# Two stages of a four-layer kernel reordered: the layer-0 attention body and the layer norm inside the layer-1 ternary feed-forward

## The chip, the cores and the metric

The kernel runs as one program on one core of a Trainium2 chip. The metric is the device time of that program in microseconds (us), as the median of several runs. The engines that matter are TensorE (PE in the profile), VectorE (DVE), ScalarE (ACT), GpSimd (POOL) and SyncE (SP, which issues the transfers). Each engine works through its own instructions in program order. Engines wait for each other on semaphores.

## The reference

The reference is a stack of four layers over `x` of 4 batches x 512 rows x 512 features, each with a cross-attention part and a feed-forward part, both added to `x` with a tanh gate. Two parts matter here.

```python
# layer 0 attention (teacher_logits is layernorm(x), teacher_features is the context)
query  = einsum('bnc,dc->bnd', teacher_features, Wq) + bq
key    = einsum('bnc,dc->bnd', teacher_features, Wk) + bk
attention = softmax(einsum('bnd,bmd->bnm', query, key), axis=-1)
x = x + tanh(g_xattn[0]) * einsum('bln,bmn->blm', teacher_logits, attention)

# layer 1 feed-forward
def act_quant(x):                       # per row, 8 bits
    scale = 128 / clip(max(abs(x), axis=-1), 1e-5)
    return clip(round(x * scale), -128, 127) / scale
def bitlinear(x, w):   return einsum('bsh,oh->bso', act_quant(x), weight_quant(w))
def h_bitlinear(x, w): return einsum('bsh,oh->bso', act_quant(fwht(x)), weight_quant(w))
x = x + tanh(g_ffn[1]) * h_bitlinear(silu(bitlinear(n, w_gate)) * bitlinear(n, w_up), w_down)   # n = layernorm(x)
```

Layer 3's attention slot is a selective scan. It needs, from the context alone, a projection, a causal convolution of four taps with silu (`u`), a small projection (`xd`) and `dt = softplus(...)`. The kernel computes these inside the layer-0 attention stage, beside the attention.

## The kernel before

The program is a chain of phases, each ended by a barrier over all engines: `setup`, `l0_xattn`, `l0_ffn`, `l1_xattn`, `l1_ffn`, `l2_xattn` and so on. The change touches `l0_xattn` (line 345), `l1_ffn` (line 1472) and the class `LayerNorm` (line 131). Inside a phase the order on each engine is written out by hand. PSUM banks are handed round by a `Ring`: a list of jobs in order, each job taking the next bank, with a semaphore for "filled" and one for "drained". A job that is to fill a bank waits until the earlier job on that bank has been drained.

**`l0_xattn`** loops over four batches b (a body). On PE a body transposes the normalised rows (`xt`), makes `q` and `k`, projects `u` to `xd` (`project_x`), makes four score tiles `e0` to `e3`, then `dt` tiles, transposes the probabilities (`pt`), and makes four output tiles `out0` to `out3`, with the input projections of the next batch (`in{b+1}_c`) in between. The score tiles wait for `q` (drained by ACT) and `k` (drained by DVE). DVE takes the maximum of each score tile, ACT takes the exponential, DVE scales, PE transposes. DVE further does the convolution of the next batch (`convolve`, four pieces c), the layer norm of the next batch and the residual additions. Softplus is a chain across three engines: ACT takes small_exp, logarithm, inverse, then GpSimd multiplies (line 671), ACT squares, and DVE closes with five passes per piece (`softplus(b, c)`, lines 611 and 615). Before the change the body of b ends on DVE with `softplus(b, 0)` and `softplus(b, 1)`, ahead of the `xt` and `k` drains of b+1, and pieces 2 and 3 come after the `pt` copies of b+1. On ACT a body ends with `gated(b + 1)`, the silu that makes `u`.

**`l1_ffn`** is a software pipeline over 16 row tiles t (T1 = 16, four per batch). In turn t, PE transposes `mid` of t-1, makes gate and up of t, transposes the quantised rows of t-3, does half of the Hadamard transform of t-1 (line 1574), the down product of t-3, and the other half of the transform. DVE in turn t does, in this order: `widest(t-2)`, which drains the transform's banks; `rest(t-2)`, three butterfly passes, the row maximum and the scale; `middle(t)`, which is silu(gate) times up; and `down(t-3)`, the residual. `widest` must drain two banks before PE can transpose the last of `mid`. ACT copies, takes the silu, and rounds the transformed rows in `y_round(t-2)`. Once per batch there is extra work for the next batch. At t % 4 == 1 DVE runs the whole layer norm behind `down`. At t % 4 == 2 it runs `quantise_x` there: the row maximum, the scale, then two clamping passes into `tmp` for each of four tiles. At t % 4 == 3 ACT turns `tmp` into the integers `xq` in one pass behind `y_round` (`x_round`). At t % 4 == 0 PE transposes `xq` and ACT copies the result to `xqt`.

Of the kernel before, what the change touches and what calls it, by code (L numbers as in the profile page):

```python
# [9 lines left out]
ALU = mybir.AluOpType  # L10
ACT = mybir.ActivationFunctionType
# [124 lines left out]
class LayerNorm:  # L136
# [10 lines left out]
    def vector(self, dve, i, batch, xn_free, xn=None, first=0):  # L147
        g, st = self.g, self.steps
        xn = g["xn"] if xn is None else xn
# [17 lines left out]
        xn_free()  # L167
# [177 lines left out]
def l0_xattn(nc, g, a, early):  # L345

    with Phase(nc, "l0x") as ph:
# [79 lines left out]
        def _(pe):  # L427
# [28 lines left out]
            for b in range(NB):  # L456
# [29 lines left out]
        def _(act):  # L486
# [36 lines left out]
            def small_exp(b):  # L523
                for c in range(DC):
# [5 lines left out]
            def logarithm(b):  # L530
                for c in range(DC):
# [3 lines left out]
            def inverse(b):  # L535
                for c in range(DC):
# [3 lines left out]
            def squares(b):  # L540
                for c in range(DC):
# [9 lines left out]
            for b in range(NB):  # L551
# [17 lines left out]
                small_exp(b)  # L569
                pad(b + 1, 2)  # L570
                logarithm(b)
                pad(b + 1, 3)
                inverse(b)
                squares(b)
                gated(b + 1)

        @blk.vector
        def _(dve):
# [42 lines left out]
            for b in range(NB):  # L621
                xt_drain(dve, "dve", g, ring, b, xt)
                ring.wait_filled(dve, b, "k")
                ring.drain(dve.tensor_scalar(kt[:], bank("k"), bias[:, 1:2], None, ALU.add), "k")
                for m in range(ST):
# [12 lines left out]
                convolve(b + 1, 0)  # L638
# [3 lines left out]
                if b > 0:  # L642
                    softplus(b - 1, 2)
                    softplus(b - 1, 3)
# [3178 lines left out]
```

## Time and profile before

| what | us |
|---|---|
| median of 3 runs (3500.46 to 3504.72) | 3502.61 |
| the profiled execution, own time | 3490.28 |
| its span, first to last instruction | 3488.6 |

In the profiled execution, `l0_xattn` runs from about 15 us to 232 us, and `l1_ffn` from 1077 us to about 1450 us. Times inside the trace are us from the start of the span. In a timeline row the first number is the start, the second the duration of the group up to the end of its last instruction, "xN" the number of instructions in it, and the bracket says how long the engine had been idle before it and what released it. Back-to-back instructions overlap a little, so busy time is not exactly elapsed time.

### The profile page before, as it was taken

How to read it: one execution, taken by the hardware profiler on the slowest of the kernel's cores; microseconds unless marked ns; L12 is line 12 of the kernel's file. 1: busy time of each engine (PE TensorE's matmuls, PEld its weight loads, DVE VectorE, ACT ScalarE, POOL GpSimd, SP SyncE). 2: the span in 40 equal slices, each digit the busy share in tenths (PEclk: the TensorE clock that was granted, in tenths of full speed). 3: DMA queues.
4: the chain of work that ended last, by engine and by line, in shares of the span. 5: the costliest groups of instructions: out<-in, count | busy, mean ns of one | idle time of the engine just before them, and what ended most of it. 6: DMA issues, size and time to landing. Idle time of an engine off the chain costs nothing. (4 is left out here: it accounts for less than half of the span.)

```text
span 3488.6 us, 42689 instructions
## 1 busy us (share of the span) xinstructions
PE 3122.0 (89%) x14213; PEld 1833.0 (53%) x14244; DVE 2621.1 (75%) x3478; ACT 1844.0 (53%) x3430; POOL 1443.2 (41%) x957
## 2 busy tenths in 40 slices
PE   7869797999997888799999999999999787998985
PEld 3437554333334555455555555555555366786663
DVE  7855689877774888468888888887788864765886
ACT  5644343666663655565666666666656432664220
POOL 1122279000000000067777777777778654223430
PEclk9879899999998999899999999999999898999998
DMA  4137735222216400245555555455454346675421
GB/s 133 40 118 277 277 103 151 58 58 58 64 32 150 63 1 1 85 153 155 182 170 167 162 189 168 154 169 180 159 171 144 127 182 211 249 254 192 145 73 60
DMA packets 229749, 478.66 MB, mean 137 GB/s; under 512 B 36239, under 2 KB 69647, under 8 KB 213664
## 3 DMA queue, kind: packets, MB, share of 16 engines
q1 hardware_dynamic: 223296, 459.19, 41.2%
q0 software_dynamic: 6240, 16.81, 1.3%
q8 instruction: 113, 1.85, 0.2%
q14 instruction: 100, 0.82, 0.1%
HBM read 387.51 MB, written 92.06 MB: 137 GB/s over the span
## 5 line engine op out<-in xcount | busy, mean ns | idle before, releaser
L2393 POOL TENSOR_TENSOR l2x_inflow<-l2x_dtu,l2x_rows_b 128x512 f32<-128x512 f32 x256 | 437.2, 1708 | 254.8 <-DVE l2x_state L2279 253.5
L178 POOL TENSOR_TENSOR ln_work<-ln_work,minus_half 128x4 f32<-128x4 f32 (+1 forms) x34 | 33.1, 975 | 1000.4 <-DVE ln_work L166 1000.3
L2279 DVE TENSOR_TENSOR_SCAN l2x_state<-l2x_decay,l2x_inflow 128x512 f32<-128x512 f32 x256 | 403.9, 1578 | 0.0
L2409 POOL TENSOR_TENSOR l2x_y_sum<-l2x_y_sum,l2x_state 128x512 f32<-128x512 f32 x224 | 387.0, 1728 | 29.2 <-DVE l2x_state L2288 29.2
L1324 DVE TENSOR_REDUCE l1x_mx<-psum 128x2 f32<-128x1024 f32 x256 | 308.4, 1219 | 96.6 <-PE psum L1166 95.2
L1281 ACT ACTIVATE l1x_split<-psum 128x1024 f32<-128x1024 f32 x256 | 262.0, 1025 | 155.6 <-PE psum L1166 155.6
L2288 DVE TENSOR_TENSOR l2x_state<-l2x_state,l2x_rows_c 128x512 f32<-128x512 f32 x256 | 298.2, 1165 | 7.1
L2151 ACT ACTIVATE l2x_decay<-l2x_dt,a_neg 128x512 f32<-128x512 f32 x256 | 181.6, 721 | 165.5 <-DVE l2x_state L2279 165.1
L126 PE MATMUL psum<-l2x_probs_t,l2x_v_tok 128*128 128x512 f32 x512 | 236.3, 605 | 16.1 <-ACT l2x_qt L212 12.9
L126 PE MATMUL psum<-l2x_xt,l2x_wq 128*128 128x512 f32 x512 | 231.9, 597 | 8.6 <-issue 8.6
L2086 ACT ACTIVATE l2x_probs<-psum,l2x_soft,l2x_norms 128x512 f32<-128x512 f32 x256 | 195.6, 774 | 79.9 <-DVE l2x_soft L2218 79.9
L126 PE MATMUL psum<-l2x_kt,l2x_qt 128*128 128x512 f32 x512 | 228.7, 593 | 0.9 <-DVE x_res L218 0.9
L126 PE MATMUL psum<-l2x_wo,l2x_ot 128*128 128x512 f32 x512 | 222.5, 592 | 0.9 <-DVE l2x_ot L2230 0.9
L126 PE MATMUL psum<-l2x_wkv,l2x_ctx_t 128*128 128x512 f32 x768 | 199.1, 415 | 8.8 <-DMA l2x_wkv<-l2x_kv_dram 8.8
L2211 DVE TENSOR_REDUCE l2x_soft<-psum 128x1 f32<-128x512 f32 x256 | 163.5, 681 | 34.9 <-PE psum L126 34.7
L126 PEld LDWEIGHTS psum<-l2x_wkv,l2x_ctx_t 128*128 128x128 f32 x768 | 146.4, 191 | 55.7 <-issue 13.9
L1190 PE MATMUL psum<-l1x_split,l1x_v 128*32 128x256 f32 x2048 | 164.2, 393 | 2.4 <-ACT l1x_o_sb L212 1.3
L126 PEld LDWEIGHTS psum<-l2x_xt,l2x_wq 128*128 128x128 f32 x512 | 96.3, 191 | 126.0 <-issue 125.8
L126 PEld LDWEIGHTS psum<-l2x_wo,l2x_ot 128*128 128x128 f32 x512 | 96.0, 190 | 116.5 <-issue 116.5
L126 PEld LDWEIGHTS psum<-l2x_probs_t,l2x_v_tok 128*128 128x128 f32 x512 | 93.2, 192 | 115.9 <-issue 93.5
L126 PEld LDWEIGHTS psum<-l2x_kt,l2x_qt 128*128 128x128 f32 x512 | 94.4, 190 | 103.6 <-issue 91.6
L119 PEld LDWEIGHTS psum<-ident,l2x_probs 128*128 128x128 f32 x1024 | 115.9, 143 | 47.5 <-issue 37.0
(459 smaller groups left out, 7147.5 us busy)
## 6 DMA issues: line engine op xcount, KB each, us to landing
l2x_rows_b<-l3x_xd_dram SPq DMA_DIRECT2D x256, 256.0 KB, 3.9
l2x_rows_c<-l3x_xd_dram SPq DMA_DIRECT2D x256, 256.0 KB, 3.5
l2w_raw<-l_w SPq DMA_DIRECT2D x38, 1024.0 KB, 6.7
l2x_wkv<-l2x_kv_dram SPq DMA_DIRECT2D x32, 1024.0 KB, 6.8
l2w_raw<-l_w SPq DMA_DIRECT2D x38, 512.0 KB, 4.7
l1x_heads_dram<-l1x_stage SPq DMA_DIRECT2D x32, 512.0 KB, 3.3
l2x_wq<-l_wq SPq DMA_DIRECT2D x16, 1024.0 KB, 5.1
l2x_wo<-l_wo SPq DMA_DIRECT2D x16, 1024.0 KB, 7.3
```

The lines of the kernel that those rows point to most:

```text
L119: last = pe.transpose(bank[:, k * P:(k + 1) * P], tile, ident)
L126: last = pe.matmul(out, lhsT, rhs, start=(k == 0), stop=(k == len(pairs) - 1))
L1190: last = pe.matmul(bank(f"o{gg}", outr)[32 * j:32 * j + 32, cols], v[:, gg // NG, kt, h * VW:h * VW + 2 * HD], probs[:, kt % 2, j, cols], ...
L1281: main.drain(act.activation(probs[:, kt % 2, 2 * j:2 * j + 2, :], g["psum"][:, b:b + 2, :], ACT.Exp, scale=HD ** -0.5), f"{job}_0", banks=2)
L1324: main.drain(dve.tensor_reduce(mx[:, gg % 2, :, j, t], g["psum"][:, b:b + 2, :], AX.X, ALU.max), f"m{n}_0", banks=2)
L2086: ring.drain(act.activation(probs[:, h % 2, t, :], bank(f"s{u}_{h}_{t}"), ACT.Exp, bias=soft[:, h, 1, t:t + 1], scale=norms[:, u % 2, 1, h ...
L2151: act.activation(decay[:, s % 3, :], dt[:, u % 2, :], ACT.Exp, scale=g["a_neg"][:, u % G2, n:n + 1]).then_inc(decay_ready, 1)
L2211: dve.tensor_reduce(soft[:, h, 0, t:t + 1], bank(f"s{u}_{h}_{t}"), AX.X, ALU.max, negate=True).then_inc(max_ready, 1)
L2279: dve.tensor_tensor_scan(state[:, s % KEPT, :], decay[:, s % 3, :], inflow[:, s % 3, :], 0.0, ALU.mult, ALU.add).then_inc(scan_done, 1)
L2288: dve.tensor_tensor(tile, tile, rows_c[:, s % 3, :], ALU.mult).then_inc(gathered, 1)
L2393: pool.tensor_tensor(inflow[:, s % 3, :], dtu[:], rows_b[:, s % 3, :], ALU.mult).then_inc(inflow_ready, 1)
L2409: pool.tensor_tensor(total, total, state[:, s % KEPT, :], ALU.add).then_inc(added, 1)
```

## The change

In `l0_xattn`, for bodies b > 0: PE makes the score tiles before `project_x`. ACT takes `gated(b)` after the `q` drain instead of at the end of body b-1, and takes `xd` after the exponentials. `project_in(b+1, 0)` and its `pad` come before the first `dt` tiles. DVE runs `softplus(b-1, 0)` behind the `xt` drains, `softplus(b-1, 1)` behind the `k` drain, pieces 2 and 3 ahead of the `pt` copies; `convolve(b+1, 0)` comes behind these copies and `convolve(b+1, 1)` into the gap in the layer norm. In the last body ACT runs the softplus chain in two halves of two pieces, and DVE runs pieces 0 and 1 ahead of the residual additions.

In `l1_ffn`: the layer norm is cut into `moments` (at t % 4 == 0) and `apply` (at t % 4 == 1). These and `quantise_x` (at t % 4 == 2) now stand between `widest` and `rest`. `quantise_x` loses its passes over `tmp`; ACT does them in `x_round`, as four scaled activations and one Relu pass that clamps, and the turned copy undoes the sign. `x_round` stands ahead of `y_round`.

```diff
@@ LayerNorm
     def vector(self, dve, i, batch, xn_free, xn=None, first=0):
+        self.moments(dve, i, batch, first)
+        xn_free()
+        self.apply(dve, i, batch, xn, first)
...
@@ l0_xattn
-            jobs += [f"xd{b}", f"dt{b}_0", f"dt{b}_1", ins[0], f"dt{b}_2", ins[1], f"dt{b}_3", ins[2], ins[3]]
+            jobs += [f"xd{b}", ins[0], f"dt{b}_0", f"dt{b}_1", f"dt{b}_2", ins[1], f"dt{b}_3", ins[2], ins[3]]
...
@@ l0_xattn, PE
-                project_x(b)
+                if b == 0:
+                    project_x(b)
                 for m in range(ST):
                     ring.wait_for(pe, b, free=f"e{m}", drained=["q", "k"])
                     ring.fill(product(pe, bank(f"e{m}"), [(qt[:, m * P:(m + 1) * P], kt[:])]))
+                if b > 0:
+                    project_x(b)
+                project_in(b + 1, 0)
                 project_dt(b, 0)
                 project_dt(b, 1)
-                project_in(b + 1, 0)
                 project_dt(b, 2)
...
@@ l0_xattn, ACT
-                take_xd(b)
+                if b > 0:
+                    gated(b)
+                if b == 0:
+                    take_xd(b)
...                                     # the four exponentials
+                if b > 0:
+                    take_xd(b)
+                pad(b + 1, 0)
                 signs(b, 0)
                 signs(b, 1)
-                pad(b + 1, 0)
...
-                squares(b)
-                gated(b + 1)
+                if b < NB - 1:
...                                     # the chain as before, over all four pieces
+                else:
+                    for pieces in ((0, 1), (2, 3)):
+                        small_exp(b, pieces)
+                        logarithm(b, pieces)
+                        inverse(b, pieces)
+                        squares(b, pieces)
...
@@ l0_xattn, DVE
                 xt_drain(dve, "dve", g, ring, b, xt)
+                if b > 0:
+                    softplus(b - 1, 0)
                 ring.wait_filled(dve, b, "k")
                 ring.drain(dve.tensor_scalar(kt[:], bank("k"), bias[:, 1:2], None, ALU.add), "k")
+                if b > 0:
+                    softplus(b - 1, 1)
...
-                convolve(b + 1, 0)
+                if b > 0:
+                    softplus(b - 1, 2)
+                    softplus(b - 1, 3)
+                else:
+                    convolve(b + 1, 0)
...                                     # pt copies
                 if b > 0:
-                    softplus(b - 1, 2)
-                    softplus(b - 1, 3)
+                    convolve(b + 1, 0)
...
-                ln.vector(dve, b, (b + 1) % NB, lambda: ring.wait_filled(dve, b, "xt3"))
-                convolve(b + 1, 1)
-                convolve(b + 1, 2)
+                def xn_free(b=b):
+                    convolve(b + 1, 1)
+                    ring.wait_filled(dve, b, "xt3")
+
+                ln.vector(dve, b, (b + 1) % NB, xn_free)
+                if b == NB - 1:
+                    softplus(b, 0)
+                    softplus(b, 1)
...                                     # out0, out1
+                convolve(b + 1, 2)
                 convolve(b + 1, 3)
...                                     # out2, out3
-                softplus(b, 0)
-                softplus(b, 1)
...
@@ l1_ffn, ACT
             def x_round(b):
                 act.wait_ge(x_ready, b + 1)
+                for s in range(ST):
+                    act.activation(tmp[:, s, :], g["xn"][:, s, :], ACT.Copy, scale=xs[:, b % 2, 2, s:s + 1],
+                                   bias=ROUND).then_inc(x_rounded, 1)
+                act.wait_ge(x_rounded, (b + 1) * ST)
...
-                act.activation(xq[:]..., tmp[:]..., ACT.Copy, bias=-ROUND).then_inc(xq_done, 1)
+                act.activation(xq[:]..., tmp[:]..., ACT.Relu, scale=-1.0, bias=top[:, 0:1]).then_inc(xq_done, 1)
...
                 if 0 <= t - 1 < T1:
                     halves(t - 1)
+                if t % ST == ST - 1 and t // ST + 1 < NB:
+                    x_round(t // ST + 1)
                 if 0 <= t - 2 < T1:
                     y_round(t - 2)
-                if t % ST == ST - 1 and t // ST + 1 < NB:
-                    x_round(t // ST + 1)
@@ l1_ffn, DVE
...                                     # quantise_x: two clamping passes per tile and their waits removed
+                b = t // ST
                 if 0 <= t - 2 < T1:
                     widest(t - 2)
+                if t % ST == 0 and t < T1:
+                    if b == NB - 1:
+                        ring.wait_for(dve, 0, drained=[f"dn{ST - 1}"])
+                    ln.moments(dve, b, (b + 1) % NB)
+                if t % ST == 1 and t < T1:
+                    dve.wait_ge(xq_done, b + 1)
+                    ln.apply(dve, b, (b + 1) % NB)
+                if t % ST == 2 and b + 1 < NB:
+                    ln.wait_xn(dve, b + 1)
+                    quantise_x(b + 1)
+                if 0 <= t - 2 < T1:
                     rest(t - 2)
                 if t < T1:
                     middle(t)
                 if 0 <= t - 3 < T1:
                     down(t - 3)
-                b = t // ST
...                                     # the layer norm and quantise_x that stood here are gone
```

## Rows read from the trace of the kernel before

**Rows 1.** The page: the span, and the busy time of each engine.
```profile
span 3488.6 us, 42689 instructions
PE 3122.0 (89%) x14213; PEld 1833.0 (53%) x14244; DVE 2621.1 (75%) x3478; ACT 1844.0 (53%) x3430; POOL 1443.2 (41%) x957
```
**Rows 2.** Busy time by stretch: length, then PE, PEld, DVE, ACT, POOL, clock, DMA share.
```profile
132.22:183.20 50.98, 43.65 (x113) 19.20 (x113) 43.73 (x72) 30.49 (x50) 7.10 (x5) 0.90 0.11 43
183.20:228.15 44.95, 26.67 (x65) 12.36 (x64) 36.29 (x63) 22.82 (x38) 7.02 (x5) 0.76 0.06 25
1077.00:1450.00 373.00, 295.23 (x1837) 190.36 (x1869) 299.28 (x432) 204.25 (x238) 4.63 (x7) 0.90 0.27 50
```
**Rows 3.** Timeline of PE in the attention: the score tiles of bodies 1, 2, 3.
```profile
79.72 3.70 PE L126 MATMUL psum<-l0x_kt,l0x_qt 128*128 128x512 f32 x8 [0.63 <-DVE l0x_kt L624]
...
132.22 3.70 PE L126 MATMUL psum<-l0x_kt,l0x_qt 128*128 128x512 f32 x8
...
183.20 3.70 PE L126 MATMUL psum<-l0x_kt,l0x_qt 128*128 128x512 f32 x8
```
**Rows 4.** Waits in the attention, 15 to 232 us: total, times, longest.
```profile
DVE l0x_conv L594 <- ACT l0x_padded L212: 12.7, 4, 4.3
```
**Rows 5.** Timeline of DVE in the attention: two convolution pieces, and the last instruction.
```profile
109.73 2.33 DVE L597 SCALAR_TENSOR_TENSOR l0x_conv<-l0x_padded,early_conv_w,l0x_conv 128x512 f32<-128x512 f32 x3
...
112.49 5.00 DVE L597 SCALAR_TENSOR_TENSOR l0x_conv<-l0x_padded,early_conv_w,l0x_conv 128x512 f32<-128x512 f32 x3
...
227.46 0.69 DVE L615 SCALAR_TENSOR_TENSOR l0x_dt<-l0x_small,l0x_relu 128x512 f32<-128x512 f32 x1
```
**Rows 6.** Timeline of ACT in the last body of the attention.
```profile
207.62 1.28 ACT L538 ACT_TABLE_LOAD   x1
208.91 2.19 ACT L538 ACTIVATE l0x_ratio<-l0x_magnitude 128x512 f32<-128x512 f32 x4
```
**Rows 7.** Waits in the feed-forward, 1077 to 1450 us.
```profile
PE psum L119 <- DVE l1f_z L1735: 41.8, 12, 6.1
```
**Rows 8.** Timeline of PE, feed-forward: the transform that closes a turn.
```profile
1156.62 1.95 PE L1574 MATMUL psum<-l1f_had,l1f_mid_t 128*128 128x128 f32 x16
...
1304.11 1.95 PE L1574 MATMUL psum<-l1f_had,l1f_mid_t 128*128 128x128 f32 x16
...
1328.23 1.95 PE L1574 MATMUL psum<-l1f_had,l1f_mid_t 128*128 128x128 f32 x16
...
1347.62 1.95 PE L1574 MATMUL psum<-l1f_had,l1f_mid_t 128*128 128x128 f32 x16
...
1364.94 1.95 PE L1574 MATMUL psum<-l1f_had,l1f_mid_t 128*128 128x128 f32 x16
...
1389.55 1.95 PE L1574 MATMUL psum<-l1f_had,l1f_mid_t 128*128 128x128 f32 x16
...
1406.87 1.95 PE L1574 MATMUL psum<-l1f_had,l1f_mid_t 128*128 128x128 f32 x16
```
**Rows 9.** Timeline of DVE in the feed-forward.
```profile
1304.98 2.28 DVE L1693 TENSOR_REDUCE l1f_xs<-xn 128x4 f32<-128x2048 f32 x1
...
1307.98 1.67 DVE L1704 TENSOR_SCALAR l1f_tmp<-xn,l1f_xs 128x512 f32<-128x512 f32 x4
...
1347.83 0.75 DVE L1759 SCALAR_TENSOR_TENSOR x_res<-psum,l1f_ys,x_res 128x512 f32<-128x512 f32 x1 [2.88 <-PE psum L126]
...
1365.81 2.46 DVE L154 BATCH_NORM_STATS2 ln_stats<-x_res 128x6 f32<-128x512 f32 x4
...
1370.52 1.92 DVE L171 TENSOR_SCALAR xn<-x_res,ln_work 128x512 f32<-128x512 f32 x4 [1.23 <-POOL ln_work L178]
...
1407.07 0.75 DVE L1759 SCALAR_TENSOR_TENSOR x_res<-psum,l1f_ys,x_res 128x512 f32<-128x512 f32 x1 [0.81 <-PE psum L126]
```
**Rows 10.** Timeline of ACT at a batch boundary of the feed-forward.
```profile
1243.91 1.89 ACT L1617 ACTIVATE l1f_xq<-l1f_tmp 128x2048 bf16<-128x2048 f32 x1
1246.52 1.94 ACT L212 ACTIVATE l1f_xqt<-psum 128x1024 bf16<-128x1024 bf16 x2 [0.71 <-PE psum L1543]
```

More of the change, by code:

```diff
@@ L147, in vector, with moments @@
     def vector(self, dve, i, batch, xn_free, xn=None, first=0):
+        self.moments(dve, i, batch, first)
+        xn_free()
+        self.apply(dve, i, batch, xn, first)
+    def moments(self, dve, i, batch, first=0):
         g, st = self.g, self.steps
-        xn = g["xn"] if xn is None else xn
         st.begin(i)
@@ L166, in vector, with apply @@
         dve.tensor_scalar(w[:, 6, :], w[:, 3, :], 0.5, None, ALU.mult).then_inc(self.var_ready, 1)
-        xn_free()
+    def apply(self, dve, i, batch, xn=None, first=0):
+        g, st = self.g, self.steps
+        xn = g["xn"] if xn is None else xn
+        w = g["ln_work"][:, :, first:first + self.tiles]
         dve.wait_ge(self.var_ready, i * 2 + 2)
@@ L521, in signs, with small_exp @@
                 side.drain(act.activation(relu[:, b % 2, c, :], bank(job, side), ACT.Relu, bias=dt_b[:, c:c + 1]), job)
-            def small_exp(b):
-                for c in range(DC):
+            def small_exp(b, pieces):
+                for c in pieces:
                     if b > 0:
@@ L528, in small_exp, with logarithm, inverse, squares @@
                     act.activation(small[:, c, :], magnitude[:, b % 2, c, :], ACT.Exp, scale=-1.0).then_inc(exp_done, 1)
[L530 to L531 removed]
+            def logarithm(b, pieces):
+                for c in pieces:
                     act.wait_ge(exp_done, b * DC + c + 1)
                     act.activation(magnitude[:, b % 2, c, :], small[:, c, :], ACT.Ln, bias=two[:, 0:1]).then_inc(ln_done, 1)
[L535 to L536 removed]
+            def inverse(b, pieces):
+                for c in pieces:
                     act.wait_ge(ln_done, b * DC + c + 1)
                     act.activation(ratio[:, c, :], magnitude[:, b % 2, c, :], ACT.Exp, scale=-1.0).then_inc(ratio_exp, 1)
[L540 to L541 removed]
+            def squares(b, pieces):
+                for c in pieces:
                     act.wait_ge(ratio_done, b * DC + c + 1)
@@ L1614, in x_round @@
                 act.wait_ge(x_ready, b + 1)
+                for s in range(ST):
+                    act.activation(tmp[:, s, :], g["xn"][:, s, :], ACT.Copy, scale=xs[:, b % 2, 2, s:s + 1],
+                                   bias=ROUND).then_inc(x_rounded, 1)
+                act.wait_ge(x_rounded, (b + 1) * ST)
                 if b >= 1:
                     ring.wait_filled(act, 0, f"xq{b - 1}_1")
-                act.activation(xq[:].rearrange("p s d -> p (s d)"), tmp[:].rearrange("p s d -> p (s d)"), ACT.Copy,
-                               bias=-ROUND).then_inc(xq_done, 1)
+                act.activation(xq[:].rearrange("p s d -> p (s d)"), tmp[:].rearrange("p s d -> p (s d)"), ACT.Relu,
+                               scale=-1.0, bias=top[:, 0:1]).then_inc(xq_done, 1)
             def x_turned(b):
@@ L1622, in x_turned @@
                     ring.wait_filled(act, 0, f"xq{b}_{k}")
-                    copy(act, "act", ring, f"xq{b}_{k}", xqt[:, b % 2, 2 * k:2 * k + 2, :].rearrange("p c n -> p (c n)"),
-                         bank_bf(f"xq{b}_{k}"))
+                    ring.drain(act.activation(xqt[:, b % 2, 2 * k:2 * k + 2, :].rearrange("p c n -> p (c n)"),
+                                              bank_bf(f"xq{b}_{k}"), ACT.Copy, scale=-1.0, bias=QMAX), f"xq{b}_{k}")
             def middle_turned(t):
@@ L1698, in quantise_x @@
                 xst.wait(dve)
+                dve.sem_inc(x_ready, 1)
                 dve.tensor_scalar(v[:, 4, :], v[:, 1, :], w_abs[:, 0, 0:1], None, ALU.mult).then_inc(scaled, 1)
                 dve.tensor_scalar(v[:, 5, :], v[:, 1, :], w_abs[:, 0, 1:2], None, ALU.mult).then_inc(scaled, 1)
-                if b >= 1:
-                    dve.wait_ge(xq_done, b)
-                for s in range(ST):
-                    xst.inc(dve.tensor_scalar(tmp[:, s, :], g["xn"][:, s, :], v[:, 2, s:s + 1], QMAX, ALU.mult, ALU.min))
-                xst.wait(dve)
-                for s in range(ST - 1):
-                    xst.inc(dve.tensor_scalar(tmp[:, s, :], tmp[:, s, :], QMIN, ROUND, ALU.max, ALU.add))
-                xst.wait(dve)
-                s = ST - 1
-                dve.tensor_scalar(tmp[:, s, :], tmp[:, s, :], QMIN, ROUND, ALU.max, ALU.add).then_inc(x_ready, 1)
             def middle(t):
@@ L1770, in _ @@
                     down(t - 3)
-                b = t // ST
-                if t % ST == 1 and t < T1:
-                    if b == NB - 1:
-                        ring.wait_for(dve, 0, drained=[f"dn{ST - 1}"])
-                    ln.vector(dve, b, (b + 1) % NB, lambda: dve.wait_ge(x_ready, b + 1))
-                if t % ST == 2 and b + 1 < NB:
-                    ln.wait_xn(dve, b + 1)
-                    quantise_x(b + 1)
         @blk.gpsimd
```

14 lines of the change are left out of this document (8 added, 6 removed).

## The prediction, on record before the result was known

> **What bounds the kernel now.** I read the page first. PE is busy 89% of the span and DVE 75% [rows 1], but these are averages over ten phases, and the change touches two. So the next view is busy time by stretch. One body of the attention, from the score tiles of batch 2 to those of batch 3, takes 50.98 us, in which PE is busy 43.65 and DVE 43.73 [rows 2]. Neither engine fills the body: each stands for some 7 us of it, waiting for the other. The feed-forward takes 373 us, with PE busy for 295 and DVE for 299 [rows 2]. Again two engines with nearly equal work take turns.
>
> The waits say where. In the feed-forward PE waited 41.8 us in 12 waits for DVE's `widest` (the last subtraction, line 1735) [rows 7]. The timeline of PE gives the rhythm. I take the start of the transform that closes each turn [rows 8]: 1304.11, 1328.23, 1347.62, 1364.94, 1389.55, 1406.87. The differences are 24.12 (the turn behind `quantise_x`), 19.39 (a batch boundary), 17.32 (plain), 24.61 (behind the layer norm), 17.32 (plain). A plain turn is PE's own loop: DVE still waits 0.81 us for the down product in it [rows 9]. Layer norm and quantisation each add about 7 us to a turn, because they stand on DVE between `down` and `widest`, exactly where PE waits for the banks.
>
> In the attention DVE's longest-lasting wait is for the padded input of the convolution, 12.7 us in four waits [rows 4], and the score tiles of bodies 1 to 3 start at 79.72, 132.22 and 183.20 [rows 3], so bodies of 52.50 and 50.98 us, and 44.95 from the last score tiles to the last DVE instruction at 228.15 [rows 3, 5].
>
> **The change part by part: feed-forward.** Nothing of the plain turn changes, so 17.32 stays. The extra pieces now stand between `widest` and `rest`, behind the drain for which PE waits. They delay `rest` and `middle`, and only what exceeds DVE's slack in that turn comes onto the path.
> - t % 4 == 1, `apply`: 1.92 us [rows 9]. DVE's slack in a plain turn is 0.81, to some 1.05 with the short wait behind `down`. So +0.8: 18.1 us. GpSimd's power, which costs a wait of 1.23 now, is a turn old by then and costs nothing.
> - t % 4 == 2, `quantise_x`: what remains runs from 1304.98 to 1307.98, 3.0 us [rows 9]. Less the slack: +2.0, so 19.3 us. The clamping passes that leave DVE are the 3.2 us that follow.
> - t % 4 == 3: plain for DVE, 17.3 us.
> - t % 4 == 0, `moments`: from 1365.81 to 1370.52 less the 1.23 of waiting, 3.5 us [rows 9]. DVE waits 2.88 at a boundary now [rows 9]. The boundary itself gets longer on ACT, which now does x_round's four activations and y_round before it copies `xqt`. Four activations of 128x512 take 2.19 [rows 6], and the Relu pass I price as today's pass, 1.89 [rows 10]. PE's transposes of `xq`, for which ACT now waits 0.71 [rows 10], are hidden beside y_round. So +2.2 - 0.7 = +1.5, which raises DVE's slack to 4.4 and covers the 3.5 of `moments`. The turn: 20.9 us. Were the four activations free it would be +0; were y_round's delay to add in full, +2.2.
>
> A batch: 20.9 + 18.1 + 19.3 + 17.3 = 75.6. Before, from 1156.62 to 1328.23 two batches took 171.61 [rows 8], so 85.8 each: two gains of 10.2. The last batch has no `quantise_x`: 20.9 + 18.1 + 17.3 + 17.3 = 73.6 against 78.64 (1328.23 to 1406.87): 5.0. In the first three turns the layer norm (3.5 + 1.2 + 1.9) and the quantisation (3.0 + 3.2) stand in line the same way, 12.8 us. DVE is the bound there, so the 3.0 that remains stays: 9, between 6 and 10. The run-out behind 1406.87 is untouched. Sum: 20.4 + 5.0 + 9 = 34 us, between 25 and 37.
>
> What queues behind the moved work: behind the longer x_round stands y_round of the same turn. Its result is wanted by PE only after the next turn's gate and up products, more than half a turn later, so the 4.1 us are hidden; without that cover they would come on top at each of three boundaries, 12 us. The start of the stage waits for weights by DMA, so the first x_round costs nothing.
>
> **The change part by part: attention.** No work leaves DVE, so a body can't be shorter than its 43.7 us of DVE work [rows 2]. What the order does is to give DVE something to do where it waits. One softplus piece is five passes of 0.69 [rows 5], 3.5 us. Piece 0 covers the time in which PE makes `q` and `k`, piece 1 the time until the first score tile, pieces 2 and 3 (7 us) the time in which ACT signs the `dt` tiles and PE transposes, and convolution 0 starts when its input has long been padded, so the 12.7 us of [rows 4] mostly go. On PE the score tiles no longer stand behind `project_x`, which waits for ACT's silu. In exchange they wait for `k` behind softplus piece 0: about 2.5 us of idle PE. Laid out by the durations of the trace, PE's own loop then takes 43 to 44, DVE's 43.7. I take 44.8, since part of PE's work will run at the lower of its two clocks as now (granted 0.90 of 2.4 GHz over body 2 [rows 2]); that puts PE some 1 us behind DVE. Bounds: 43.7 and 50.
>
> - Body 1: 52.50 to 44.8, -7.7. Body 2: 50.98 to 44.8, -6.2.
> - Score tiles of body 1: one softplus piece (3.5) moves from ahead of them to behind them, and body 0 gains about 1.5 where convolution 0 no longer waits for its padding: -5.
> - Last body: DVE has 36.3 us of work in its 44.95 [rows 2]. It gets the 3.5 that moved behind the score tiles, 39.8. It keeps the 1.2 wait for GpSimd in the layer norm and about 1 us before piece 0 of its own softplus: 42, -3. The halves add two table loads of 1.28 [rows 6] to ACT, which lie ahead of pieces 2 and 3, while DVE does pieces 0 and 1 and four residuals. Without this cover they would cost 2.6.
> - GpSimd's multiplies will still slow DVE next to them: three convolution passes took 5.00 instead of 2.33 [rows 5]. I leave that as it is, +-3 us in all.
>
> Sum: 7.7 + 6.2 + 5 + 3 = 22 us, between 10 and 27. SP's stores of `u`, `xd` and `dt` keep their order and have slack; the last store still follows the last softplus.
>
> The row of a table load shows it at 207.62 for 1.28 us and the next activation at 208.91, right behind it [rows 6]. The Trainium skill, "ScalarE: Activation LUTs", section "What ACT_TABLE_LOAD costs", puts a switch at about 2.66 us, since a drain comes on top of the load. By that rule two more switches cost 5.3 us instead of 2.6, of which my layout hides about 2, and the total would be some 3 us worse. The trace doesn't agree: it has no such gap.
>
> **Sum.** 34 + 22 = 56 us. The profiled execution took 3490.28 (span 3488.6), so it would come to 3434. The median of the runs stands 12.3 above it, at 3502.61. I apply the same difference: 3447 us.
>
> **The rivals.**
> - *Only the feed-forward gains.* In the attention PE's granted clock and the new wait for `k` eat the gaps: three bodies at 50 us. For it: DVE and PE are equally loaded, and each new order has new handovers. Against: DVE's waits of [rows 4] have a clear cause. Time: 3502.6 - 34 = 3469.
> - *Only the attention gains.* If `rest` and y_round are late for PE's transposes, each inserted piece (3.5 + 1.9 + 3.0 a batch) comes back onto the path. Against: the down product's wait shows slack only of 0.81, but the y rows are made most of a turn ahead. Time: 3502.6 - 22 = 3481, less what the removed 3.2 us save.
> - *Slower: the attention falls to the lower clock.* PE stands before every set of score tiles, and in the last body, which has such gaps, the granted clock is 0.76 [rows 2]. If bodies 1 to 3 ran at 0.6, PE's 43.65 us at 0.90 would become 65.5, with 3.5 of waiting 69 against 51: +18 a body, +54, less 34: 3523. It decides from about 0.67, where +11 a body eats the feed-forward's 34. Against: today's body 2 keeps 0.90 with as much idle time as the new one.
> - *The change doesn't do what it says:* PE's loop in both stages has other links that I missed, and all comes back as waits: within 7 us of 3502.6.
>
> **How the numbers follow.** Forecast, both stages gain (3436 to 3458): 0.76. Only the feed-forward: 0.12. Only the attention: 0.06. Nothing: 0.03. Lower clock: 0.03. Range: from the best case of both terms (37 + 27 = 64, less 2 for the runs' spread: 3436) to the feed-forward alone, 3470. About 0.2% (7 us) is what a measurement of this kernel can tell from no change. Faster 0.94, same 0.03, slower 0.03.
>
> **What would show it.** In the profile after: the waits of PE for `widest` fall from 41.8 to a few us; turns of 17.3, 18.1, 19.3 and 20.9 between the closing transforms; `xqt` copies right behind y_round at a boundary; bodies of about 45 us between score tiles, and convolution 0 without a wait; the last softplus pass of the attention near 205. I am wrong in the feed-forward if plain turns are no longer 17.3 or the y transposes wait for ACT, and in the attention if PE's waits before the score tiles are well over 3 us or its clock there is below today's.

## The result and the profile after

The changed kernel takes 3452.74 us (median of 4 runs, 3448.78 to 3460.69), against 3501.53 before in the same session. The ratio is 0.9866, 95% interval 0.9843 to 0.9888: 48.8 us less. The forecast was 3447, and 56 us less. The profiled execution took 3448.78.

The page after; as [rows 1]:
```profile
span 3447.1 us, 42710 instructions
PE 3117.6 (90%) x14244; PEld 1829.8 (53%) x14244; DVE 2600.7 (75%) x3446; ACT 1857.3 (54%) x3448; POOL 1444.7 (42%) x957
```
The busy sums hardly move (PE -4, DVE -20, ACT +13), while the span falls by 41.5. What went is idle time, so the waits and the turns tell more than the sums.

The score tiles of the attention after, from PE's timeline, as [rows 3], then DVE's last instruction, as in [rows 5]:
```profile
36.86 3.70 PE L126 MATMUL psum<-l0x_kt,l0x_qt 128*128 128x512 f32 x8
75.71 3.70 PE L126 MATMUL psum<-l0x_kt,l0x_qt 128*128 128x512 f32 x8 [1.07 <-DVE l0x_kt L648]
120.14 5.40 PE L126 MATMUL psum<-l0x_kt,l0x_qt 128*128 128x512 f32 x8 [2.32 <-DVE l0x_kt L648]
166.01 3.70 PE L126 MATMUL psum<-l0x_kt,l0x_qt 128*128 128x512 f32 x8 [2.32 <-DVE l0x_kt L648]
...
207.84 0.69 DVE L637 SCALAR_TENSOR_TENSOR l0x_dt<-l0x_small,l0x_relu 128x512 f32<-128x512 f32 x1
```
Bodies 1 and 2 went from 52.50 and 50.98 to 44.43 and 45.87 us. The last part, from the last score tiles to the end of the last softplus pass, went from 44.95 to 42.52. The attention ends at 208.53 instead of 228.15: 19.6 us earlier, where 22 were forecast. The new wait for `k` is there, in brackets.

The waits in the attention after, 15 to 232 us (total, times, longest), where the first is that of [rows 4]:
```profile
DVE l0x_conv L616 <- ACT l0x_padded L220: 4.1, 1, 4.1
PE psum L126 <- DVE l0x_kt L648: 5.7, 3, 2.3
```
The 4.1 us that are left for the padded input are at 21.34, ahead of the first score tiles; between the bodies that wait is gone.

The feed-forward's closing transforms, as [rows 8] (L1574 is now L1609), from that of turn 3 to that of turn 7:
```profile
1132.80 1.95 PE L1609 MATMUL psum<-l1f_had,l1f_mid_t 128*128 128x128 f32 x16
...
1155.73 1.95 PE L1609 MATMUL psum<-l1f_had,l1f_mid_t 128*128 128x128 f32 x16
...
1173.05 1.95 PE L1609 MATMUL psum<-l1f_had,l1f_mid_t 128*128 128x128 f32 x16
...
1191.30 1.95 PE L1609 MATMUL psum<-l1f_had,l1f_mid_t 128*128 128x128 f32 x16
...
1210.76 1.95 PE L1609 MATMUL psum<-l1f_had,l1f_mid_t 128*128 128x128 f32 x16
```
The turns are 22.93 (boundary), 17.32 (plain), 18.25 (`apply`), 19.46 (`quantise_x`). The next two boundaries take 21.24 and 22.92, and the other turns repeat to 0.01. From the stage's first load to the closing transform at 1362.83 (before: 1406.87) it is 303.06 us instead of 329.51: 26.5 less, where 34 were forecast. PE's waits there, as [rows 7]:
```profile
PE psum L119 <- DVE l1f_z L1765: 8.7, 18, 0.5
PE psum L119 <- ACT l1f_xqt L1662: 7.8, 6, 2.4
PE psum L119 <- DVEq L1754: 7.4, 4, 5.1
```
The 41.8 us in 12 waits for `widest` have become 8.7 in 18, none over 0.5. Two waits have grown. One is for `xqt`, 2.35 and 0.26 us at each of three boundaries, where none was over 0.3 before. The other is for DVE's `middle` (line 1754): `quantise_x` now stands ahead of it, and at the start of the stage, where DVE has no slack, PE waits 5.10 us for it in turn 3. Before, that wait was one of 1.0 us:
```profile
PE psum L119 <- DVEq L1724: 1.0, 1, 1.0
```

### The profile page after: what moved, and what is told of

Same layout as the page of the kernel before. It is cut to its first block and busy times, and to the rows that moved or that the text cites. A ratio compares the mean times of both kernels' runs of the same rounds, so it can differ in the third digit from the quotient of the medians.

```text
span 3447.1 us, 42710 instructions
## 1 busy us (share of the span) xinstructions
PE 3117.6 (90%) x14244; PEld 1829.8 (53%) x14244; DVE 2600.7 (75%) x3446; ACT 1857.3 (54%) x3448; POOL 1444.7 (42%) x957
## 3 DMA queue, kind: packets, MB, share of 16 engines
q1 hardware_dynamic: 223296, 459.19, 41.8%
```

## The experiments

Below, "the stage" is the feed-forward from its first load to the closing transform one turn ahead of the last one named above: 312.2 us before, 285.7 after. Kernels marked "one execution" ran once. The same code can differ by some us between executions: the seven kernels here that have the changed feed-forward (the changed kernel, e1 and a1 to a5) took 282.9 to 285.8 for this stage. From the closing transform of turn 3 on they agree within 0.1 us, so nearly all of that spread lies in the first four turns.

**e1_ffn_only.** The feed-forward's part of the change alone; `l0_xattn` is that of before.

> The feed-forward part of the change alone, attention as before. If the two parts are independent, the feed-forward stage keeps what it has with the whole change (303.1 us from its first instruction to the closing transform of turn 15, against 329.5 before) and the attention keeps its 228; median about 26 below before, so near 3476. If one stage's order or clock carries over into the other, the stage would be off by more than 2 us.

Measured: 3473.07 (4 runs), ratio 0.9931 [0.9905, 0.9957], 28.6 us less. The attention is as before (bodies 52.81 and 50.91), the stage is 284.0. The theory of independent parts holds.

**e2_attn_only.** The attention's part alone; `l1_ffn` is that of before.

> The attention part alone, feed-forward as before. Independent parts: the last softplus of the attention ends near 208.5 (228.2 before), the feed-forward stage is 329.5 again, the median about 20 below before, near 3482. The two medians' gains add up to the whole change's 49 within the runs' spread of some 5.

Measured: 3474.13 (6 runs), ratio 0.9933 [0.9915, 0.9952], 27.5 us less. Bodies 44.30 and 44.36, last part 42.41, the stage 313.1. The gain is larger than the 20 expected, and than the 18.1 us by which the attention ended earlier in the profiled execution (at 210.07). The two halves add up to 56.1 against 48.8 for the whole. Each of the three gains has an interval of some 6 to 9 us to either side, so no interaction is seen. Both rivals with one half without gain fall.

**e3_old_place.** The feed-forward's extra pieces back behind `down`; ScalarE still rounds, so the clamping passes stay gone. ("..." marks lines left out.)
```diff
                     widest(t - 2)
-                if t % ST == 0 and t < T1:
...
-                    ln.moments(dve, b, (b + 1) % NB)
-                if t % ST == 1 and t < T1:
...
-                    ln.apply(dve, b, (b + 1) % NB)
-                if t % ST == 2 and b + 1 < NB:
...
-                    quantise_x(b + 1)
...
                     down(t - 3)
+                if t % ST == 1 and t < T1:
...
+                    ln.vector(dve, b, (b + 1) % NB, lambda: dve.wait_ge(xq_done, b + 1))
+                if t % ST == 2 and b + 1 < NB:
...
+                    quantise_x(b + 1)
```


> The whole change, but layer norm and quantisation stand behind the down residual again, in one piece each; the rounding stays on ScalarE. Theory (the place is what gains): the layer-norm turn is 24.6 again, the quantisation turn 24.1 - 3.2 = 20.9, the boundary 21.2 to 22.9, a plain turn 17.3, a batch 84 to 86, and the stage up to the closing transform of turn 15 about 323 to 327, so next to nothing of the 26 us is left. Rival (the 3.2 us a batch taken off VectorE is what gains, here counted with what hangs on it): the stage stays below 312.

Measured (one execution): 3474.63; the stage 315.1, so nothing of its gain is left. PE's waits in it:
```profile
PE psum L119 <- DVE l1f_z L1765: 35.2, 18, 5.9
PE psum L119 <- ACT l1f_xqt L1662: 7.8, 6, 2.4
```
The wait for `widest` is back. The turns are 21.2 to 22.9 (boundary), 17.3 (plain), 24.8 to 25.9 (behind the layer norm) and 20.1 to 21.5 (behind `quantise_x`). DVE is rid of 3.2 us of passes a batch, which makes the last of these 2.8 to 4.0 shorter than before; the boundary, with the passes on ScalarE, is 1.8 to 3.5 longer. The theory's side is right, though the stage up to turn 15 took 332.4, over its 323 to 327.

**e4_dve_passes.** The reverse: the new place, with the clamping passes on DVE and one rounding pass on ScalarE behind `y_round`, as before. The main part of its edit:
```diff
...
+                for s in range(ST):
+                    xst.inc(dve.tensor_scalar(tmp[:, s, :], g["xn"][:, s, :], v[:, 2, s:s + 1], QMAX, ALU.mult, ALU.min))
...
-                for s in range(ST):
-                    act.activation(tmp[:, s, :], g["xn"][:, s, :], ACT.Copy, scale=xs[:, b % 2, 2, s:s + 1], bias=ROUND)
```


> The whole change, but the clamping passes are VectorE's again and ScalarE rounds in one pass behind y_round, as before; the pieces stand at their new places. Theory (the place gains): the boundary is 19.4 again, the turn with apply 18.3, the turn with quantisation 17.3 - 1.0 + 6.2 = 22.5, plain 17.3, a batch 77.5 against 76.3 to 78.0 with the change, the stage 302 to 306. Rival (the passes taken off VectorE gain): the stage is above 315.

Measured (one execution): 3462.87; the stage 288.5, 24 of the 26 us. The boundaries take 19.39, the turns behind them 17.65, the `quantise_x` turns 23.4 and 25.0, where 22.5 was expected. Moving the passes to ScalarE takes 4 to 5.5 us from one turn and puts 2 to 3.5 on another.

**e5_y_first.** On every fourth turn `y_round` stands ahead of `x_round`.
```diff
-                if t % ST == ST - 1 and t // ST + 1 < NB:
-                    x_round(t // ST + 1)
                 if 0 <= t - 2 < T1:
                     y_round(t - 2)
+                if t % ST == ST - 1 and t // ST + 1 < NB:
+                    x_round(t // ST + 1)
```


> The changed kernel, with ScalarE's two rounding helpers swapped on every fourth turn of the ternary feed-forward: y_round of the turn stands ahead of x_round of the next batch. Theory (the boundary turn is set by ScalarE's queue, in which the four scaled activations and the Relu pass, 2.57 + 2.00, delay the next evictions of h, and by the transposes of xqt behind them): the Relu pass of y, 2.00, and its move now stand ahead of x's, so xqt comes about 2 us later, TensorE waits about 2 us longer at each boundary, and the boundary turn goes from 21.2 to 22.9 up to 23 to 25; plain, quantise and apply turns stay at 17.3, 19.4 and 18.3; the stage from its first load to the closing transform of turn 14 goes from 285.7 to about 291 to 294. Rival (the order of the two is free, since both have slack and the boundary is set by the layer norm on VectorE): no turn differs by more than 0.3 and the stage stays at 286.

Measured (one execution): 3454.08; boundaries 24.17, 23.26, 23.95 (+1.0 to +2.0, +4.3 in all), all turns between and behind them the same. The boundaries lie in the range expected, with somewhat over half of the 2 us each on average: the boundary does hang on when `xqt` is made. The stage, 288.1, is below the 291 to 294 expected, also because its first four turns took 71.1 here and 73.0 in the changed kernel.

**e6_gaps.** The four scaled activations leave ScalarE's block; each stands behind one silu of the last turn of a batch.
```diff
             def x_round(b):
-                act.wait_ge(x_ready, b + 1)
-                for s in range(ST):
...
+                    if s == ST - 1 and b + 1 < NB:          # behind silu n of turn t
+                        if n == 0:
+                            act.wait_ge(x_ready, b + 2)
+                        x_scaled(b + 1, n)
```


> The changed kernel, with the four scaled activations of x_round taken out of its block and set one by one behind the silus of the last turn of a batch; its Relu pass stays in its place. Theory (the boundary is set by ScalarE's block of 2.57 + 2.00 between two sets of evictions, and by the wait for xqt that ends TensorE's activity and lowers its clock): xqt comes 2 to 2.6 us earlier, TensorE's waits of 2.35 at the boundaries go, the clock stays at its upper level behind them, and the boundary turn goes from 21.2 to 22.9 down to 19.3 to 20.5; the stage to turn 14's closing transform from 285.7 to 277 to 281. Rival (the scaled activations between silus delay each silu by 0.64, and with it the elementwise product and the next transforms, on a turn that TensorE sets): the last turn of each batch is 1 to 2.6 longer in exchange, and the stage stays at 285 to 287.

Measured (one execution): 3441.12; all three boundaries 18.66, the turns right behind them 18.38 (+1.06), the last turn of a batch unchanged, the stage 275.7. That is 10.0 us better, of which 2.1 lie in the first four turns (71.0), within what those turns vary by with the changed kernel's feed-forward. From turn 3 on it is 7.9 us better, where all executions of the changed feed-forward agree.

The +1.06 is DVE's slack used up, and not the rival's delayed silus. Here is DVE's first residual behind the first boundary, in the changed kernel and in e6:
```profile
1155.93 0.75 DVE L1789 SCALAR_TENSOR_TENSOR x_res<-psum,l1f_ys,x_res 128x512 f32<-128x512 f32 x1 [3.02 <-PE psum L126]
...
1149.52 0.75 DVE L1796 SCALAR_TENSOR_TENSOR x_res<-psum,l1f_ys,x_res 128x512 f32<-128x512 f32 x1
```
In the long boundary DVE waits 3.02 us for it, so the 3.5 us of `moments` are covered. In the short one it waits for nothing, and what `moments` has too much comes onto the next turn. The same kernel was timed again over several executions:

> The kernel with the four scaled activations between the silus of the last turn of a batch, timed in rounds (its one look gave 3441.1, with a stage 10.0 us shorter than the changed kernel's 285.7 and layer norms, attention and layer-1 mixer as there). Theory (the boundaries were the part of the feed-forward's forecast that was missing): a median of 3438 to 3446, a ratio to before of 0.982 to 0.984, and the boundary turns again at 18.4 to 19.0. Rival (the one look was a lucky execution): 3449 to 3456, as the changed kernel.

Measured: 3443.82 (4 runs, 3435.22 to 3446.61), ratio 0.9855 [0.9838, 0.9871]; boundaries 18.65 to 18.66, the stage 277.3. Its median and its boundaries are in the range expected, its ratio is just above it. Its median is 8.9 below the changed kernel's, but the kernel before ran 7.7 faster beside it too, and the intervals of the two ratios overlap. The 7.9 us behind turn 3 are 8.0 here; that the whole kernel is faster than the changed one isn't shown. Of the timed kernels it has the lowest ratio.

ScalarE at the first boundary, in its timeline, the changed kernel:
```profile
1130.04 2.57 ACT L1651 ACTIVATE l1f_tmp<-xn,l1f_xs 128x512 f32<-128x512 f32 x4
1132.64 2.00 ACT L1656 ACTIVATE l1f_xq<-l1f_tmp,l1f_top 128x2048 bf16<-128x2048 f32 x1
1134.55 1.99 ACT L1689 ACTIVATE l1f_z<-l1f_z,l1f_ys 128x2048 f32<-128x2048 f32 x1
1136.57 2.00 ACT L1693 ACTIVATE l1f_yq<-l1f_z,l1f_top 128x2048 bf16<-128x2048 f32 x1
1138.48 1.92 ACT L1662 ACTIVATE l1f_xqt<-psum 128x1024 bf16<-128x1024 bf16 x2
```
And with the gaps filled (b1_gaps_5), where the closing transform starts at 1132.65:
```profile
1120.57 0.69 ACT L1678 ACTIVATE l1f_silu<-psum,l1f_xs 128x512 f32<-128x512 f32 x1 [1.16 <-PE psum L126]
1121.16 0.71 ACT L1649 ACTIVATE l1f_tmp<-xn,l1f_xs 128x512 f32<-128x512 f32 x1
1122.35 0.69 ACT L1678 ACTIVATE l1f_silu<-psum,l1f_xs 128x512 f32<-128x512 f32 x1 [0.48 <-PE psum L126]
...
1129.89 2.02 ACT L1656 ACTIVATE l1f_xq<-l1f_tmp,l1f_top 128x2048 bf16<-128x2048 f32 x1
1131.78 2.02 ACT L1693 ACTIVATE l1f_z<-l1f_z,l1f_ys 128x2048 f32<-128x2048 f32 x1
1133.83 2.00 ACT L1697 ACTIVATE l1f_yq<-l1f_z,l1f_top 128x2048 bf16<-128x2048 f32 x1
1135.74 1.00 ACT L1662 ACTIVATE l1f_xqt<-psum 128x1024 bf16<-128x1024 bf16 x1
```
The first `xqt` copy starts 3.1 us behind the closing transform instead of 5.7. What PE does with that, first in the changed kernel:
```profile
1139.54 0.66 PE L119 MATMUL psum<-ident,l1f_mid 128*128 128x128 f32 x4 [2.35 <-ACT l1f_xqt L1662]
1140.45 0.66 PE L119 MATMUL psum<-ident,l1f_mid 128*128 128x128 f32 x4 [0.26 <-ACT l1f_xqt L1662]
1140.94 1.71 PE L126 MATMUL psum<-l1f_w_gate,l1f_xqt 128*128 128x512 bf16 x4
1142.44 1.91 PE L126 MATMUL psum<-l1f_w_up,l1f_xqt 128*128 128x512 bf16 x4
```
Then with the gaps filled:
```profile
1137.71 0.66 PE L119 MATMUL psum<-ident,l1f_mid 128*128 128x128 f32 x4 [0.24 <-ACT l1f_xqt L1662]
...
1139.08 1.03 PE L126 MATMUL psum<-l1f_w_up,l1f_xqt 128*128 128x512 bf16 x4
1139.94 1.03 PE L126 MATMUL psum<-l1f_w_gate,l1f_xqt 128*128 128x512 bf16 x4
```
Behind the waits of 2.35 and 0.26 four matmuls take 1.91 us, the lower of the clock's two levels; behind 0.24 they take 1.03, the upper. The second boundary of the changed kernel has the same two waits, and its matmuls take 1.03: it is the one of 21.24 us.

**a1_k_first.** The attention with the eviction of `k` ahead of the first softplus piece.
```diff
-                if b > 0:
-                    softplus(b - 1, 0)
                 ring.wait_filled(dve, b, "k")
                 ring.drain(dve.tensor_scalar(kt[:], bank("k"), bias[:, 1:2], None, ALU.add), "k")
                 if b > 0:
+                    softplus(b - 1, 0)
                     softplus(b - 1, 1)
```


> The changed kernel, with the first piece of the previous body's softplus chain behind the eviction of k in VectorE's order instead of ahead of it. Theory (VectorE sets the bodies of the layer-0 attention): TensorE's wait for k of 2 to 3 us a body goes, VectorE's work is the same, and the bodies stay at 44.4 and 45.9 within 1 us. Rival (the wait of TensorE for k is on the path): the two middle bodies get 1.5 to 2.5 shorter each, 3 to 5 in all, and the first score tile of the next bodies comes as much earlier.

Measured (one execution): 3463.68; bodies 46.46 and 45.44, last part 47.91. It is worse, as neither said. Waits in its last part:
```profile
ACT l0x_probs L572 <- DVE l0x_neg_max L652: 4.0, 1, 4.0
PE psum L126 <- ACT l0x_xd L220: 3.7, 1, 3.7
```
The piece now stands with its neighbour ahead of the first maximum, ScalarE's exponentials wait 4.0 us for that (2.2 in the changed kernel), `xd` behind them is late, and PE waits 3.7 for it. With `k` first PE still waits 0.85 us for it at each body, where it waited 1.07 to 2.32. So a piece ahead of `k` costs PE 0.2 to 1.5 us; behind it, it costs the softmax chain more.

**a4_dve_order and a5_pe_act_order.** The attention's new order split by engine: VectorE's alone (TensorE and ScalarE as before, last chain undivided), and its complement (a5), of whose diff against the changed kernel this is a part; its remainder restores the rest of VectorE's order.
```diff
                 xt_drain(dve, "dve", g, ring, b, xt)
-                if b > 0:
-                    softplus(b - 1, 0)
                 ring.wait_filled(dve, b, "k")
...
-                if b > 0:
-                    softplus(b - 1, 2)
-                    softplus(b - 1, 3)
-                else:
-                    convolve(b + 1, 0)
+                convolve(b + 1, 0)
```


> The changed kernel, with VectorE's half of the attention's new order alone: TensorE's and ScalarE's orders in the layer-0 attention are those of before, and the last softplus chain is undivided. The feed-forward is as in the changed kernel. Theory (the wait of 12.7 for the padded tiles, which ScalarE filled late, was most of what the attention lost, and VectorE's and ScalarE's orders have to move together): with ScalarE's order of before the padded tiles still come late, the bodies are 48 to 53, and the attention keeps at most 5 of the 20 us. Rival (VectorE's order alone, which puts other work ahead of the convolution, fills the wait): bodies of 44 to 47 and at least 12 of the 20 kept.

> The complement of the run with VectorE's new order alone: TensorE's and ScalarE's new orders in the layer-0 attention and the last softplus chain in halves, with VectorE's order of before. The feed-forward is as in the changed kernel. VectorE's order alone had kept the bodies at 41.6, 44.2, 44.4 and the last at 42.9. Theory (VectorE's order is what brought the gain; what ScalarE fills early helps only where VectorE is not held by the convolution ahead of its other work): bodies of 48 to 52 and an end of the attention within 6 us of before's 228. Rival (either side by itself ends the wait of 12.7 for the padded tiles, since an earlier fill removes it as well as a later convolution): bodies of 44 to 46 here too.

Measured (one execution each): a4 3449.14, bodies 44.18 and 44.42, last part 42.91, attention over 17.7 us earlier than before. a5 3493.27, bodies 55.19 and 56.50, last part 52.64, attention over 15.8 us later than before. VectorE's order alone brings 17.7 of the 19.6; my theory for a4, at most 5, was wrong. Without it the other half does harm, more than my theory for a5 said (bodies of 48 to 52, an end within 6 us). The bodies of a5 by stretch, columns as [rows 2], then body 1 of the kernel before, then two waits of a5:
```profile
79.61:134.80 55.19, 47.98 (x112) 21.13 (x113) 42.88 (x72) 30.73 (x50) 7.41 (x5) 0.84 0.08 33
134.80:191.30 56.50, 46.91 (x112) 20.83 (x112) 43.90 (x72) 31.03 (x51) 7.19 (x5) 0.85 0.10 39
...
79.72:132.22 52.50, 47.72 (x112) 20.91 (x112) 42.90 (x72) 30.22 (x49) 7.53 (x5) 0.84 0.10 42
```
```profile
PE psum L126 <- DVE l0x_kt L646: 11.9, 3, 5.0
DVE l0x_conv L616 <- ACT l0x_padded L220: 10.2, 3, 4.0
```
My reading is that DVE has `k` behind its long tail of softplus and convolution while PE, in the new order, has nothing else to do until `k` is there. In body 2 the granted clock is 0.85 instead of 0.90 [rows 2] and PE is busy 3.3 us longer, which is part of the 5.5 us that the body lost; body 1 had 0.84 before too, so there its 2.7 us are not the clock's. Only in body 2 does something of the "slower" rival's mechanism show.

**a2_no_halves.**
```diff
-                    for pieces in ((0, 1), (2, 3)):
+                    for pieces in (range(DC),):
```


> The changed kernel with the last softplus chain undivided: all four magnitudes, logarithms, inverses and squares in one set each. Theory (the halves are worth little, since two more table loads of 1.28 go in and VectorE waits 2.43 for the squares in the middle): the last body, from its score tiles to the end of the last softplus, goes from 42.5 to between 42 and 43.5. Rival (the halves give what the forecast put on them, a third of the last body's gain): 44.5 or more.

Measured (one execution): 3452.89, last part 46.59, 4.1 more. The rival is right, and more than right. DVE's timeline behind the layer norm without the halves:
```profile
195.00 1.02 DVE L633 SCALAR_TENSOR_TENSOR l0x_small<-l0x_magnitude 128x512 f32<-128x512 f32 x1 [4.66 <-ACT l0x_magnitude L554]
196.05 3.31 DVE L633 SCALAR_TENSOR_TENSOR l0x_small<-l0x_small,l0x_magnitude 128x512 f32<-128x512 f32 x2
```
And in the changed kernel:
```profile
191.40 1.08 DVE L633 SCALAR_TENSOR_TENSOR l0x_small<-l0x_magnitude 128x512 f32<-128x512 f32 x1 [2.43 <-ACT l0x_magnitude L554]
192.51 1.42 DVE L633 SCALAR_TENSOR_TENSOR l0x_small<-l0x_small,l0x_magnitude 128x512 f32<-128x512 f32 x2
```
The wait is 2.2 longer, and two passes run into GpSimd's multiplies (3.31 instead of 1.42). In a4, also undivided, but with the old orders of ScalarE and TensorE, that chain starts 13.8 us behind the last score tiles instead of 17.5, and the last part is 42.91. So the halves mostly repay what the new orders of these two engines cost.

**a3_pool_small.** GpSimd multiplies 8 of 512 columns, so most of that product is left out.
```diff
-                    pool.tensor_tensor(r, r, small[:, c, :], ALU.mult).then_inc(ratio_done, 1)
+                    pool.tensor_tensor(r[:, 0:8], r[:, 0:8], small[:, c, 0:8], ALU.mult).then_inc(ratio_done, 1)
```


> The changed kernel, in which GpSimd multiplies only 8 of 512 columns of each softplus ratio (this leaves out most of that product). Theory (VectorE and GpSimd stand in each other's way where their passes read two tiles in SBUF: the convolution's three passes took 4.99 to 5.18 instead of 2.33 beside GpSimd's products): the passes at the slow places take 2.3 to 2.6, and the two middle bodies are 2 to 4 shorter each, at 41 to 43. Rival (the slow passes are hidden by other waits in the body): passes faster, bodies within 0.7 of 44.4 and 45.9.

Measured (one execution): 3457.61; the slow passes at 2.33, but bodies 44.31 and 44.36, last part 41.05. The rival is right. Here are its two middle bodies, columns as [rows 2]:
```profile
80.07:124.38 44.31, 42.73 (x113) 19.45 (x113) 39.90 (x73) 30.28 (x51) 2.71 (x5) 0.92 0.12 49
124.38:168.74 44.36, 42.73 (x112) 19.44 (x112) 39.88 (x73) 30.27 (x51) 2.69 (x5) 0.92 0.12 49
```
And those of b1_gaps_5, which has the changed kernel's attention whole:
```profile
77.82:122.12 44.30, 42.73 (x112) 19.43 (x112) 41.55 (x73) 30.46 (x51) 7.21 (x5) 0.92 0.12 49
122.12:166.49 44.37, 42.73 (x113) 19.45 (x113) 41.56 (x73) 30.48 (x51) 7.20 (x5) 0.92 0.12 49
```
DVE loses 1.65 us of work a body and the body doesn't move: GpSimd's interference isn't on the path there, only in the last part (1.3 us).

## Why the prediction was right, and where its sizes were off

The time lies inside the range and the mechanism is the one forecast; e1 and e2 show that both stages gain, e3 and e4 that the place is what gains in the feed-forward.

- **Turns.** `apply` 18.25 for 18.1, `quantise_x` 19.46 for 19.3, plain 17.32 for 17.3. Counting DVE's slack and letting only the excess through was right to 0.2 us.
- **Boundary.** The mis-sized term. Forecast 20.9; measured 21.24 once and 22.9 twice, +4.4 us in all. The scaled activations took 2.57 for 2.19 and the Relu pass 2.00 for 1.89, which covers the +0.3. The other 1.7 come twice, where PE's clock fell behind the wait for `xqt`. I had priced the late copy as delay only, not what an idle PE loses afterwards. In e6 and b1 the wait and the loss go together, and the boundary comes to 18.66, below even the 19.39 of before. `moments` was hidden, as forecast: it can delay only the turn behind the boundary, and that stayed at 17.32. But it was the long boundary that hid it, as the prediction's sum has it (slack of 4.4 for 3.5): where the boundary is 19.39 (e4) the turn behind it takes 17.65, where it is 18.66 (e6) it takes 18.38.
- **First turns** (0 to 3). Forecast 9, although the prediction's own rows make it 12.8 - 3.0 = 9.8. Measured 6.2 (79.26 to 73.03). With this same feed-forward the part takes 70.2 to 70.4 in a1, a2 and a3, 71.2 in e1, 72.9 in a4 and 73.1 in a5; with that of before it takes 80.0 in e2. So the gain lies between 6.2 and 9.7, by the pair of executions that one takes, and the forecast is inside. Between the changed kernel and a2 the granted clock in the stage's first 34 us differs, and a2's first transposes of `mid` come 2.0 us earlier, reckoned from the stage's start. The windows:

The changed kernel:
```profile
1059.77:1093.77 34.00, 20.84 (x99) 10.65 (x100) 13.44 (x28) 15.35 (x20) 1.61 (x4) 0.75 0.96 278
```
a2_no_halves:
```profile
1067.03:1101.03 34.00, 21.02 (x115) 12.34 (x118) 14.16 (x28) 16.24 (x22) 1.61 (x4) 0.80 0.99 289
```
- **Attention.** Middle bodies 44.8 forecast; 44.43 and 45.87 in the profiled execution, 44.18 to 44.42 in five others with VectorE's new order (e2, e6, b1, a2, a4), 44.65 and 44.43 in e3, and a second body of 45.87 and 46.06 in two more (e4, e5). The 45.87 begins with score tiles at the lower clock, 5.40 instead of 3.70 us, behind a wait of 2.32 for `k`; the next score tiles have the same wait and take 3.70. The first body gave 3.6 (and its start 0.4) for the 5 forecast, the last part 2.4 for 3. The reasoning for the length was partly wrong: I took it from DVE's 43.7 of work with PE 1 us behind, but a3 takes 1.65 of it away, and a body with PE busy 42.73 at a clock of 0.92 lasts as long as one of 44.43 with 39.69 at 1.00. Neither engine's sum sets it; some chain of handovers does, and no run says which.
- **Covers.** The halves' table loads were hidden, as forecast: DVE starts piece 2 right behind the residuals, without a wait.
```profile
201.44 0.68 DVE L633 SCALAR_TENSOR_TENSOR l0x_small<-l0x_magnitude 128x512 f32<-128x512 f32 x1
```
One load starts at 184.79 and the next activation at 186.09, 1.30 later, so the 1.28 each that I took for a load held. Ahead of piece 0 DVE waits 2.43, where I had about 1. That this edit is worth 4.1 us in the new order, and mostly makes good what the reordering of ScalarE and TensorE costs, I had not seen. Nor had I priced the orders of the engines apart: 17.7 of the 19.6 us come with VectorE's.
- **The rest.** The stages in between and behind, which the change doesn't touch, took 4.6 us more in this profiled execution than in that of before. The gain of the medians is 48.8, that of the spans 41.5, and that of the two stages 46.
- **Luck in the total.** The forecast median, 3447, is only 6 us below the measured one. The profiled execution was forecast at 3434 and took 3448.78, 15 us more: 10 from the two stages and 4.6 from the rest. Most of that vanished in the last step. I added the 12.3 us by which the median of before stood above its profiled execution; for the changed kernel that difference is 4.0.

## What to carry to other kernels

Where two engines take turns, look for the drain that the other one waits for, and put independent work behind it, never ahead of it: e3 and e4 show that the place was worth 24 to 29 us and the move of 3.2 us of passes a batch to ScalarE, as one block, 3 us at most. A helper engine's block at a batch boundary is priced by when its last output is wanted, and its pieces may fit one by one into that engine's gaps: cut up like that (e6), the same move was worth 9.5 us from turn 3 on, against 1.6 as a block. A wait of a few us on TensorE can cost again behind it (here 1.7 us behind waits of 2.6 in all), so count both. Slack that hides a piece goes when the turn gets shorter: `moments` came onto the path as soon as the boundary was mended. Orders of several engines belong together: the half of a reordering that looks harmless cost 16 us by itself.

## What the hardware showed

- In the feed-forward PE was at its lower clock behind waits of 2.35 and 0.26 us at two of three boundaries (four matmuls in 1.91 instead of 1.03 us), with +1.7 us each time. With waits up to 0.45 at the same place (e6, b1) it stayed at the upper level at all three. Which boundary keeps the clock changed between executions.
- Four activations 128x512 with a scale per row took 2.57 us in a row, 0.71 each by themselves; over 2048 columns one pass takes 2.00.
- Two passes of DVE that read two tiles in SBUF took 3.31 instead of 1.42 us beside GpSimd's multiply; the convolution's three, 4.11 to 5.18 instead of 2.33 in the changed kernel. With GpSimd's multiply cut to 8 columns (a3) the convolution's took 2.33.
